# A message-passing kernel on one core: the projection stages written out, with their gathers and their normalisation rearranged

## What is computed

```python
def _layernorm(x, axis=-1, eps=1e-05):
    m = jnp.mean(x, axis=axis, keepdims=True)
    v = jnp.var(x, axis=axis, keepdims=True)
    return (x - m) / jnp.sqrt(v + eps)

h = jnp.maximum(_layernorm(x), 0.0)
# layer 0, m = 0, 1, 2
h = h + sigmoid(gat_conv(h, src, dst, Ws[m], att_src[m], att_dst[m], bias[m], n))
# gat_conv and layer 2: project, score, softmax over the edges of a node, weighted sum
hw = h @ W;  s = hw @ a_src;  d = hw @ a_dst
```

## Time and profile before

| | us |
|---|---|
| median of 3 runs | 4023.5 (4010.86 to 4040.4) |
| profiled execution | 4039.1, its span 4037.4 |
| P0, first instruction (L1290) to the next stage | 203.0 |
| P1 | 210.8 |
| P2 | 205.4 |
| P4 | 206.9 |
| busy: PE, DVE, ACT, POOL | 2352.2, 2246.1, 1625.7, 2168.0 |

### The profile page before, as it was taken

How to read it: one execution, slowest core, us unless ns; L and a number is a source line. 1 busy time by engine, 2 the same in 40 slices (tenths; PEclk the granted TensorE clock), 3 DMA queues, 4 the chain that set the end, 5 groups by cost and what they waited for, 6 DMA issues and landing times. The chain is left out here.

```text
span 4037.4 us, 57894 instructions
## 1 busy us (share of the span) xinstructions
PE 2352.2 (58%) x13633; PEld 1865.0 (46%) x13633; DVE 2246.1 (56%) x7631; ACT 1625.7 (40%) x3515; POOL 2168.0 (54%) x1921
## 2 busy tenths in 40 slices
PE   1136899899897664455646557775635433444333
PEld 1023676667677553354546445444624322333222
DVE  4145998899997665323422448885676323333223
ACT  0006999999995663222422323323421222222100
POOL 3628765566554770152055245555820488788755
PEclk9998999999999786587678668887866666666666
DMA  2140132233321543642455363333413433332243
GB/s 62 28 174 24 43 97 91 85 108 90 95 68 45 135 129 86 160 115 78 127 145 138 86 178 99 93 89 89 113 29 90 119 72 72 73 73 64 50 142 113
DMA packets 569016, 380.34 MB, mean 94 GB/s; under 512 B 51389, under 2 KB 511942, under 8 KB 568386
## 3 DMA queue, kind: packets, MB, share of 16 engines
q1 hardware_dynamic: 510050, 329.99, 27.7%
q0 software_dynamic: 56000, 46.29, 6.1%
q10 hardware_dynamic: 2720, 1.23, 0.2%
HBM read 249.08 MB, written 153.32 MB: 100 GB/s over the span
## 5 line engine op out<-in xcount | busy, mean ns | idle before, releaser
L1147 POOL DMA_INDIRECT p_ends_state<-t_d,p_ends_ix x300 | 315.6, 1052 | 543.9 <-issue 243.7
L806 POOL TENSOR_TENSOR a_rs<-a_ve,w_neg_half 128x16 f32<-128x16 f32 x113 | 330.4, 2924 | 244.8 <-DVE a_ve L742 214.9
L1367 PE MATMUL p_pm<-w_aug,p_ht 128*128 128x130 f32 (+1 forms) x1600 | 331.8, 329 | 173.0 <-ACT p_ht L1321 117.2
L832 ACT ACTIVATE a_nr<-a_xb,a_nm,a_rs 128x128 f32<-128x128 f32 x882 | 371.6, 490 | 26.1 <-POOL a_nm L808 26.1
L1367 PEld LDWEIGHTS p_pm<-w_aug,p_ht 128*128 128x128 f32 x1600 | 275.7, 234 | 194.9 <-issue 137.3
L1983 POOL DMA_INDIRECT e_a<-t_d,e_ix x200 | 211.7, 1059 | 269.7 <-DMA e_a<-t_s 206.9
L894 PE MATMUL a_ps<-w_ident,a_nr 128*128 128x128 f32 x1568 | 248.1, 282 | 127.8 <-ACT a_ht L840 46.9
L902 PE MATMUL a_ps<-a_ht,w_aug 128*128 128x512 f32 x588 | 315.6, 622 | 2.4 <-DVE a_ht L709 2.4
L894 PEld LDWEIGHTS a_ps<-w_ident,a_nr 128*128 128x128 f32 x1568 | 181.6, 144 | 276.7 <-issue 245.1
L709 DVE TENSOR_TENSOR a_ht<-a_ps,a_ht 128x512 f32<-128x512 f32 x294 | 203.1, 694 | 137.4 <-ACT a_ps L847 119.2
L1708 PE MATMUL c_pq<-layer_src,c_sel 128*128 (+1 forms) x800 | 194.3, 420 | 126.7 <-ACT c_sel L1679 83.5
(11 more groups left out here) (359 smaller groups left out, 6657.2 us busy)
## 6 DMA issues: line engine op xcount, KB each, us to landing
t_s<-p_ends_state SPq DMA_DIRECT2D x100, 256.0 KB
c_a<-t_d SPq DMA_DIRECT2D x100, 256.0 KB
t_d<-c_a SPq DMA_DIRECT2D x100, 256.0 KB
a_xa<-in_x SPq DMA_DIRECT2D x98, 256.0 KB
out<-a_xb SPq DMA_DIRECT2D x98, 256.0 KB, 2.0
p_ends_state<-t_s SPq DMA_DIRECT2D x75, 256.0 KB
p_ends_state<-t_d SPq DMA_DIRECT2D x75, 256.0 KB
t_acc<-q_zt SPq DMA_DIRECT2D x3, 2171.5 KB
```

Of the source, the lines that this page charges most:

```text
L806: nc.gpsimd.tensor_tensor(RS[:, z, :], VE[:, z, :], w["neg_half"][:, None, 0:J].to_broadcast([P, LNS, J]), ALU.pow).then_inc(s_rstd.sem, 1)
L832: last = nc.scalar.activation(NR[k][:, T.at(NORM[k], 2), cols(j)], normed_rows(T, k)[:, cols(j)], ACT.Identity, bias=NM[:, T.at(1, SHORT), ...
L1147: eng.indirect_dma_start(out=self.A[:, g, SRC, j, :], out_offset=None, in_=self.t[self.dst_table], in_offset=bass.IndirectOffsetOnAxis(ap= ...
L1367: last = nc.tensor.matmul(PM[side][:, j, 0:CW], HT[:, g, side, j * C:(j + 1) * C], rhs, start=side == SRC, stop=True)
```

## The change

It touches `project` and what it needs, and `rows_found`.

- The streams of `project` are written out for all 25 blocks; no loop, no register, no `carry_waits`. The state ring is RING = 7 deep; `HT`, `UP`, `XS` and the moments have SHORT = 3 places.
- Gathers take their index straight from `map_ix` or `map_at`. Each of four lanes j has a semaphore; gather j of a block waits for the landing of gather j of the block before. POOL does nothing else. In P0 the map rows go straight to `f["found"]`, now int32, on lanes of their own, and `rows_found` converts them with `tensor_copy`.
- A new class `Moments` takes (var + eps) to the power -0.5 with an initial value from the bits of the float and three Newton steps, 13 small DVE operations on 128x8, placed between the stats and aggregates of the next block.
- ACT normalises both halves, with the ReLU in the same instruction in P0. DVE keeps both products and adds the bias (`hold`); the bias matmuls and ACT's copy go.
- The order on DVE in turn n is, with norm: stats(n) with Newton(n-1), residual(n-4), hold(n-3); without: residual(n-1) and hold(n), residual first. SP's order is store(b), load(b+6).

```diff
...
+        "found": sb("found", [P, T, WORDS], I32),
...
+            done(v.tensor_copy(k["map_ix"][:, :], f["found"][:, :, 0]))
+            done(v.tensor_copy(OWNER[:, :], f["found"][:, :, 1]))
             for j in range(1, J):
-                done(v.tensor_tensor(OWNER[:, :], OWNER[:, :], f["found"][:, 0:T, 1 + j], ALU.min))
+                done(v.tensor_copy(TMP[:, :], f["found"][:, :, 1 + j]))
+                done(v.tensor_tensor(OWNER[:, :], OWNER[:, :], TMP[:, :], ALU.min))
...
+    def newton(self, eng, b, step):
...
+        v, g = self.nc.vector, b % self.ring
+        ve, half, square, y = self.var_eps[:, g, :], self.half[:, g, :], self.square[:, g, :], self.rstd[:, g, :]
+        if step == 0:
+            eng.wait_ge(self.s_moments, b + 1)
+            v.tensor_scalar(ve, self.moments[:, g, :, 1], LN_EPS, None, ALU.add).then_inc(self.s_newton, 1)
+            return
+        eng.wait_ge(self.s_newton, b * (self.STEPS - 1) + step)
+        if step == 1:
+            v.tensor_scalar(half, ve, -0.5, None, ALU.mult)
+            v.tensor_scalar(y.bitcast(I32), ve.bitcast(I32), -0.5, 1597463007.0, ALU.mult, ALU.add).then_inc(self.s_newton, 1)
+        elif step == self.STEPS - 1:
+            v.scalar_tensor_tensor(self.shift[:, g, :], self.moments[:, g, :, 0], -1.0, y, ALU.mult, ALU.mult).then_inc(self.s_shift, 1)
+        elif step % 3 == 2:
+            v.tensor_tensor(square, y, y, ALU.mult).then_inc(self.s_newton, 1)
+        elif step % 3 == 0:
+            v.tensor_tensor(square, square, half, ALU.mult).then_inc(self.s_newton, 1)
+        else:
+            v.scalar_tensor_tensor(y, square, 1.5, y, ALU.add, ALU.mult).then_inc(self.s_newton, 1)
...
+    def turn(self, eng, rows, b, last):
...
+        v = self.nc.vector
+        step = 0
+        for n in range(self.n):
+            if b <= last:
+                ins_ = v.bn_stats(self.stats[:, b % self.ring, n, :], rows(n))
+                if n == self.n - 1:
+                    ins_.then_inc(self.s_stats, 1)
+            if b and step < self.STEPS:
+                self.newton(eng, b - 1, step)
+                step += 1
+        if b <= last:
+            eng.wait_ge(self.s_stats, b + 1)
+        for n in range(self.n):
+            if b <= last:
+                ins_ = v.bn_aggr(self.moments[:, b % self.ring, n, :], self.stats[:, b % self.ring, n, :])
+                if n == self.n - 1:
+                    ins_.then_inc(self.s_moments, 1)
+            if n % 2 and b and step < self.STEPS:
+                self.newton(eng, b - 1, step)
...
 def project(nc, w, k, t, r, heads, rhs, bias_row, kind, plus_x, keep, f=None):
...
+    first, normed = kind == "first", kind == "normed"
+    sigmoid, norm, overlay = not normed, kind != "plain", not first
+    RING, SHORT = 7, 3
...
+        A = sb("a", [P, RING, 2, J, C])
+        HT = sb("ht", [P, SHORT, 2, J * C])
+        NR = HT[:, :, :, :].rearrange("p g s (j c) -> p g s j c", j=J)
+        UP = sb("up", [P, SHORT, J, C]) if sigmoid else None
+        XS = sb("xs", [P, SHORT, J, C]) if plus_x else None
...
+            def load(b):
+                g = b % RING
+                if b >= RING:
+                    eng.wait_ge(s_out[g], (uses(b) - 1) * OUTS)
+                    eng.wait_ge(s_mm[DST], b - RING + 1)
+                for side in (SRC, DST):
+                    eng.dma_start(A[:, g, side, :, :], block_rows(t[tables[side]], b)).then_inc(s_load[g], 16)
...
+            def store(b):
+                g = b % RING
+                if first:
+                    eng.wait_ge(s_normed[DST], b + 1)
                     eng.dma_start(block_rows(t["d0"], b), A[:, g, DST, :, :]).then_inc(s_out[g], 16)
-                wait(eng, s_next, b + 1)
-                carry_waits(eng, w)
+                eng.wait_ge(s_next, b + 1)
...
-            stream(eng, (load, 0), (store, 4))
...
+            for b in range(RING):
+                load(b)
+                if plus_x and b < SHORT:
+                    load_x(b)
+            for b in range(BLOCKS):
+                store(b)
+                if b and b - 1 + RING < BLOCKS:
+                    load(b - 1 + RING)
+                if plus_x and b + SHORT < BLOCKS:
+                    load_x(b + SHORT)
+            for g in range(RING):
+                eng.wait_ge(s_out[g], OUTS * len(range(g, BLOCKS, RING)))
...
+            @block.gpsimd
+            def _(eng):
+                for b in range(BLOCKS):
+                    g = b % RING
+                    eng.wait_ge(s_load[g], uses(b) * 32)
+                    for j in range(J):
+                        if b:
+                            eng.wait_ge(s_over[j], 16 * b)
+                        eng.indirect_dma_start(out=A[:, g, SRC, j, :], out_offset=None, in_=t[f"d{r}"],
+                                               in_offset=bass.IndirectOffsetOnAxis(ap=k["map_ix"][:, b * J + j:b * J + j + 1], axis=0),
+                                               bounds_check=EP - 1, oob_is_err=False).then_inc(s_over[j], 16)
+        if first:
+            @block.gpsimd
+            def _(eng):
+                for n in range(T):
+                    lane, turn = n % J, n // J
+                    if turn:
+                        eng.wait_ge(s_found[lane], 16 * turn)
+                    eng.indirect_dma_start(out=f["found"][:, n, :], out_offset=None, in_=t["maps"].rearrange("(n a) o -> n (a o)", a=WORDS),
+                                           in_offset=bass.IndirectOffsetOnAxis(ap=f["map_at"][:, n:n + 1], axis=0),
+                                           bounds_check=NODES - 1, oob_is_err=False).then_inc(s_found[lane], 16)
+                for lane in range(J):
+                    eng.wait_ge(s_found[lane], 16 * (T // J))
...
+        def there(eng, b, side=None):
...
+            g = b % RING
+            if overlay and side != DST:
                 for j in range(J):
...
+                    eng.wait_ge(s_over[j], 16 * (b + 1))
+            eng.wait_ge(s_load[g], uses(b) * 32)
 
...
-            steps = []
-            if ends.overlay:
-                steps.append((lambda b, g: ends.index(eng, b, g), 0))
-            if kind == "first":
-                steps += [(map_index, 0), (found, 5)]
-            if norm:
-                lag = 2 if kind == "first" else 3
-                steps += [(stats, lag), (product, 4), (apply, lag), (residual, 4)]
-            else:
-                steps += [(residual, 3), (product, 2)]
...
+            def hold(b):
+                for side in (SRC, DST):
+                    eng.wait_ge(s_mm[side], b + 1)
+                    v.tensor_tensor(held(("src", "dst")[side], b)[:, :, 0:CW], PM[side][:, :, 0:CW], wide, ALU.add).then_inc(s_keep[side], 1)
...
+            def residual(b):
...
+                there(eng, b, SRC)
+                v.tensor_tensor(A[:, g, SRC, :, :], A[:, g, SRC, :, :], grow, ALU.add).then_inc(s_next, 1)
+            holds, residuals = (3, 4) if norm else (0, 1)
+            for n in range(BLOCKS + residuals):
+                if norm and n <= BLOCKS:
+                    if n < BLOCKS:
+                        there(eng, n)
+                    mo.turn(eng, lambda m: A[:, n % RING, m // J, m % J, :], n, BLOCKS - 1)
+                if 0 <= n - residuals:
+                    residual(n - residuals)
+                if 0 <= n - holds < BLOCKS:
+                    hold(n - holds)
 
...
+            def apply(b):
+                g, m = b % RING, b % SHORT
+                eng.wait_ge(mo.s_shift, b + 1)
+                if normed and b >= SHORT:
+                    eng.wait_ge(s_mm[DST], b - SHORT + 1)
                 for side in (SRC, DST):
-                    wait(eng, nb.s_normed[side], (b + 1) * J)
-                    nc.scalar.activation(A[:, g, side, :, :], A[:, g, side, :, :], ACT.Relu).then_inc(s_relu, 1)
...
+            copies, squashes = (1, 2) if norm else (0, 1)
+            for n in range(BLOCKS + squashes):
+                if norm and n < BLOCKS:
+                    apply(n)
+                if 0 <= n - copies < BLOCKS:
+                    copy(n - copies)
+                if sigmoid and 0 <= n - squashes:
+                    squash(n - squashes)
 
...
-            def product(b, g):
+            def product(b):
...
+                    eng.wait_ge(s_ht, b * 2 + side + 1)
+                    if b:
+                        eng.wait_ge(s_keep[side], b)
                     for j in range(J):
-                        if side == DST:
-                            nc.tensor.matmul(PM[side][:, j, 0:CW], w["ident"][:, :], BR[:, :], start=True, stop=False)
-                        last = nc.tensor.matmul(PM[side][:, j, 0:CW], HT[:, g, side, j * C:(j + 1) * C], rhs, start=side == SRC, stop=True)
-                    last.then_inc(s_mm, 1)
...
-            stream(eng, (turn, 0), (product, 0))
+                        last = nc.tensor.matmul(PM[side][:, j, 0:CW], HT[:, b % SHORT, side, cols(j)], rhs, start=True, stop=True)
```

(13 more changed lines are left out.)

185 lines of the change are left out of this document (60 added, 125 removed).

## The result

The changed kernel took 4076.0 us (median of four runs, 4070.5 to 4085.7), the kernel before 4019.0 (4010.9 to 4040.4): a ratio of 1.013, 95% interval 1.010 to 1.016. The forecast was 3856, range 3822 to 3920. It is 1.3% slower, not faster. A later pair on another chip gave 4078 against 4025, ratio 1.013 (1.009 to 1.017); a pair on yet another chip gave 3793 against 3836, ratio 0.989 (0.986 to 0.992). What separates these two results is the subject of what follows.

A forecast was written before the change was run, and what follows sets the result against it. POOL was taken to bound P0 and P4 (root and gathers), late index copies P1 and P2. Gains 65 + 56 + 45 + 1.6 = 167.6 bring 4037.4 to 3869.8, less 13.9 profile excess: 3856 us, range 3822 to 3920.

The forecast's parts named there:

- What bounds P1 and P2 before: P1, P2: gathers held by DVE's late index copy, behind older blocks' arithmetic; POOL waits 2.3 us a block in P1.
- PE keeps up behind POOL: P1, P2: PE needs at most 4.5 us a block with hand-overs, under the gathers' 5.2.
- 1.30 us a gather sets the stage: P1, P2: POOL's gather pace decides, 99 x 1.30 = 128.8 us; stages 146 and 149, gains 65 and 56.
- rival D: P1, P2: PE's late results add 2.3 us a block, 6.8 in all; +80, total 3936 us; chance 0.10.
- its 100 gathers ... hidden behind DVE: P0: POOL's gathers take 130 us, covered by DVE's turns of 5.8 us; stage 156.8, gain 46.
- rival C: P0, P4: Newton steps not hidden, each shows 0.22 us, P0's turn 7.4; +54, total 3910 us; chance 0.13.
- P4's loop through the ring: P4: store, load, gathers and residual take 15.6 us per two turns, 7.8 a block; stage 205.3, gain 1.6.
- The bound of 4.4: P4's loop: load issue to gather start, 4.4 us from loads at 1681.46, where 3.7 was taken and 2.46 was low.
- The recorded low sum of this loop, 13.3: P4: lowest price of the ring loop for two turns, 6.7 us a block, against 15.6 taken and 18.9 high.
- Rival B, the lanes: P1, P2: gather landings pass 5.2 us or queue, 6.2 a block; +50, total 3906 us; chance 0.11.
- The slower rival (E): P1, P2: PE's lateness strikes every block; slower kernel once it passes 4.1 us, 4064 at 4.9; chance 0.04.
- A's bounds: Range of the summed case A (3856 us, chance 0.62) from the stages' low and high terms: 3822 to 3900.

The follow-up runs named there:

- e1: Changed kernel, P0's gathers moved to rows_found (P0 156.7 us), P1 without lanes (190.8), P4 with pow back on POOL (221.5); total 4079 against 4006 before.
- e6: Changed kernel; P0 gathers out of bounds (265.3 us); P1 small additions; P2 waits for landings (242.9); P4 pow back, ring 10; total 4234 against 4037 before.
- e8: Changed kernel, idle pow on POOL every 6 gathers in P0 and P4, 12 in P1, 16 in P2; P4 ring 10: 3901 us against 3991 before.
- e2: Changed kernel, idle pow on POOL after every four gathers in P0, P1, P4, every gather in P2: P0 184.5 us, total 4130 against 4006 before.
- e12: Changed kernel untouched, on a chip where gather streams delay nobody: 3793 us against 3836 for the kernel before, ratio 0.989.
- e13: Changed kernel, idle pow every 6 gathers in P0 and P4, 12 in P1 and P2, P4 ring 10, on e12's chip: 3804 us against 3836 before.
- e3: Changed kernel; P0's gathers moved out, 80 POOL pows instead (156.9 us); P1, P4 memset after each gather; P2 pow every four; total 4113 against 4006 before.

## Why the prediction was wrong, step by step

- **What bounds P1 and P2 before** was misread. The rows were right: gathers stood for the index, the index for PE's late results. The step that failed is that PE keeps up behind POOL, so that "1.30 us a gather sets the stage", with the late results priced only as rival D, "what holds P1 and P2 lies in PE", with its "a stop of 9 us is made up if PE's mean is under 5.2". D took the late results as a thing of PE that comes so often, whatever POOL does. The runs showed that POOL's stream makes them (P0 in e1 and e6; in P1 breaks on POOL give 166.0, e8) and the rows that they ended when POOL waited. So the more of the change works, the more results are late. P1 and P2 got 20 and 24 us, not 65 and 56.
- **P0: "its 100 gathers ... hidden behind DVE"** put the price of running beside the others at nothing. They cost 103 us (260.1 against 157.3 or 156.7). In the kernel before pow broke the stream after every four gathers, for 2 us; with such a pow put back, P0 falls to 184.5 (e2). What I counted as POOL's burden was what kept the others going. The total of that sum held without the delay, 156.8 forecast, 156.7, 156.9 and 157.3 measured, but in part by luck. On the chip of e12 residuals follow one another at 5.4 us on average where 5.8 was taken, some 9 us less over the stage, and the stage ends 10.3 us after the issue of its last store at 1382.66 where 3.4 was taken; what holds that end is not shown. Newton between the stats cost less than the 0.10 a step that was taken: from the stats of 1304.84 to the residual of 1308.08 it is 3.24 us, 0.76 over the 2.48 of stats and aggregates, 0.06 a step. So rival C fell, and with it the first rule of the Trainium skill, page "VectorE: DVE Perf Modes", section "The DRAIN you can't avoid", by which the turn would have been 6.8; the trace disagrees with it here, and agrees with the section's own exception that a next operation which is not held starts earlier.
- **P4's loop through the ring** was the right mechanism with a term too small. The chip of e12 shows it undisturbed. DVE's residuals (L1358) and the stats between, SP's store and load, POOL's first and fourth gather:

```profile
2616.03 0.69 DVE L1358 TENSOR_TENSOR p_a<-p_a,layer_src 128x512 f32<-128x512 f32 x1
```

```profile
2616.75 0.38 SPq L1284 DMA_DIRECT2D t_s<-p_a  x1
2617.23 0.45 SPq L1271 DMA_DIRECT2D p_a<-t_s  x1
```

```profile
2623.42 1.00 POOL L1308 DMA_INDIRECT p_a<-t_d,k_map_ix  x1 [7.35 <-DMA p_a<-t_d]
...
2627.32 1.00 POOL L1308 DMA_INDIRECT p_a<-t_d,k_map_ix  x1 [0.31 <-DMA p_a<-t_d,k_map_ix]
```

```profile
2629.94 0.29 DVE L1203 BATCH_NORM_STATS2 p_mo_st<-p_a 128x6 f32<-128x128 f32 x1 [6.35 <-DMA p_a<-t_d,k_map_ix]
```

  Residual end to store 0.03, store to load 0.48, load to gather 6.19, three spacings 3.90, last landing 2.62, stats to residual's end at 2634.19 4.25: 17.5 for two blocks. From the stats of block 8 to those of block 24 it is 140.2 us, 8.8 a block, where 7.8 was forecast. The forecast had 0.1, 0.4, 3.7, 3.9, 3.0 and 4.5 = 15.6. The load is the term: 6.19 here, 4.7 to 6.8 in this stage's other loads from block 7 on, where I took 3.7. The bound of 4.4 was itself counted from the second of the block's two loads; from the first, at 1681.02, it is 4.8. It also came from a moment without a store, while these loads come right behind a store of 256 KB on the same queue; that the store is what delays them is likely, but no run takes it away. The slower loop makes +15 of the +18 us by which 223.4 misses 205.3. The delay adds another 14 to 24 on the first kind of chip (237.8, 246.9). A ring of 10 brings P4 to 192 to 195 where a pow after every five or six gathers keeps the stream apart. The recorded low sum of this loop, 13.3, is also a little off: 0.5, 2.46, 3.9, 2.46 and 4.4 make 13.7.
- **Rival B, the lanes**: nothing on the first chip (e1). On the chip of e12 the streams are longer than forecast: P1's lasts 135.8 us from first to last gather instead of 128.8, P2's 142.9. That is the size of the 7 and 13 us by which e12 misses 146 and 149. The profile puts the longest of these waits, 1.6 us, to the landing of a gather, which would be B in small; no run without lanes on such a chip shows it.
- **The range** took in no case with P0 above its old time, because no row showed gathers without a break beside other work for longer than P1's 16, and I did not ask what the pow was doing for the others. The slower rival (E) put the late results into P1 and P2 only, and at every block. (A's bounds, 3822 to 3900, do not follow from its terms either: 19, 3 and 6 down and 27, 15 and 20 up give 3828 to 3918. The measured 4076 is outside both.)
- Measured against the windows on the chip without the delay, the forecast sum of the four stages, 657 us, stands against 695.6; but the gain there is small for another reason: the kernel before is faster by 92 us in P1 and P2 (150.5, 174.1). The change gains 39 us there, 735.0 to 695.6: 45 in P0, 12 in P2, nothing in P1, and P4 loses 16.

## What to carry to other kernels

An engine that issues indirect DMAs without a pause is not always free for the others, even if they share no data with it: before such a stream is made denser, look for results that arrive late while it runs and in time when it stops, and where they do, try a pause of one or two microseconds every 6 to 12 gathers; where they don't, it only costs (10 to 19 us a stage in e13). A wait that ends a stall is not its cause: if A waits for B and B gets going when A stops, removing the wait does not free B. And measure both kernels on more than one chip when the change moves how gathers and compute overlap.

## What the runs showed of the hardware

- On the chips that delay, POOL's indirect DMAs, issued 1.30 us apart, make many hand-overs late, of DVE by about 4 us and of PE by 7 to 20 and more, also when no row is moved (e6, P0 265.3), and not when POOL computes instead (e3, 156.9). Others in the same stream are prompt: ACT's normalisations from 1406.19 on were used by PE at 1407.88, DVE's product of 1429.28 by ACT at 1430.01, and chained DVE steps start 0.3 us apart at 1385.30 to 1385.92. What tells the late from the prompt ones was not found. A break of 0.37 us does little in P0 (243.3), one of about 1.6 us every 4 to 8 gathers takes most of the loss away there (172.9 to 185.9), idle time ends the late results too (e6, P2). What inside the chip is held was not settled. The Trainium skill, page "SBUF — State Buffer", section "Who interferes with whom", knows a lock between DVE and GpSimd for certain operations. By that section PE never waits on it, while PE's results are the latest here, and e3's pow stream, which reads and writes the same memory, delays nobody; so the lock alone does not explain it.
- The delay is a property of the chip, or of its condition at the time, that came in two kinds and nothing between: the keys stage at 250 or 179 us, P0 of the same program at 260 or 157. What distinguishes the chips is open.
- Loads issued 0.48 us behind a store of 256 KB on the same queue let their gather start 4.7 to 6.8 us later (e12, P4), against 4.4 to 5.0 for the first load of a stage, with no store ahead.
